# A fused decoder layer: the head norm's weights and residual on VectorE, the second norm and the choice of experts one or two tiles sooner

## What is computed

```python
x = _layernorm(x + _L0_attn_ref(x, ...))            # a state space scan
x = _layernorm(x + _L0_xattn_ref(x, ctx, ctx, ...)) # mLSTM, 4 heads of 64, queries from x, keys and values from ctx
x = _layernorm(x + _L0_ffn_ref(x, ...))             # 8 experts, each token uses 2
```

```python
h = jnp.einsum('bnst,bntd->bnsd', C / (normalizer + EPS_BACKEND), vh)
mean = h.mean(-1, keepdims=True)
var = h.var(-1, keepdims=True)
hn = (h - mean) * jax.lax.rsqrt(var + NORM_EPS) * outnorm_weight
# residual and layernorm, then:
logits = x @ gate_w
mult, sel = _sparse_mixer_routing(logits)   # the two best of 8 experts, and their gates
out = jnp.einsum('etf,efh,te->th', silu(x @ w1) * (x @ w3), w2, w)
```

## Time and profile before

| what | us |
|---|---|
| median of 3 runs (800.7 to 806.85) | 802.03 |
| the profiled execution | 804.1 |
| its span in the profile | 802.6 |
| TensorE busy | 678.2 (84%) |
| VectorE busy | 432.3 (54%) |
| ScalarE busy | 242.4 (30%) |
| GpSimd busy | 279.9 (35%) |

### The profile page before, as it was taken

One profiled execution on the slowest core, in us unless ns is written; L12 is line 12 of the kernel. 1 busy time (PEld: TensorE's weight loads), 2 busy tenths in 40 slices (PEclk: granted clock), 3 DMA queues, 4 the chain that ended last, 5 costly groups with the idle time before them and its releaser, 6 DMA issues.

```text
span 802.6 us, 13999 instructions
## 1 busy us (share of the span) xinstructions
PE 678.2 (84%) x3863; PEld 543.1 (68%) x3864; DVE 432.3 (54%) x1243; ACT 242.4 (30%) x473; POOL 279.9 (35%) x203
## 2 busy tenths in 40 slices
PE   6999879999957887843399999999999999999910
PEld 2566658887535665633288888888888888888810
DVE  3666673365435686797354454554445454455526
ACT  3444431111124844314032423223332323222204
POOL 7000010000102255766920272716463173710036
PEclk9998875599996977875599999999999999999965
DMA  9000017000210000412340004040414104000054
GB/s 288 14 0 2 0 49 162 1 0 1 112 46 1 1 2 0 178 57 90 120 185 27 26 26 183 26 183 26 183 33 183 33 27 183 26 28 27 26 181 146
DMA packets 33524, 57.88 MB, mean 72 GB/s; under 512 B 13328, under 2 KB 28432, under 8 KB 32208
## 3 DMA queue, kind: packets, MB, share of 16 engines
q1 hardware_dynamic: 24368, 42.88, 15.6%
q0 software_dynamic: 3360, 9.25, 3.2%
q10 hardware_dynamic: 5760, 5.33, 2.4%
HBM read 44.90 MB, written 12.54 MB: 72 GB/s over the span
## 4 chain that ended last, share of the span: by engine, by line
PE 70%; DVE 13%; POOL 6%; ACT 4%; issue 3%; DMA 2%; POOLq 0%; DVEq 0%; SPq 0%; ACTq 0%
PE bank L1944 25%; PE bank L1964 12%; PE bank L1634 6%; PE bank L1754 4%; PE bank L1954 4%; PE bank L1739 3%; POOL experts_w L760 3%; PE bank L1742 2%; PE bank L1644 2%; PE bank L1863 1%; DVE small L1205 1%; PE bank L1774 1%; PE bank L1824 1%; POOL small L647 1%; PE bank L1930 1%
## 5 line engine op out<-in xcount | busy, mean ns | idle before, releaser
L1944 PE MATMUL bank<-experts_w,experts_x 128*128 x912 | 231.1, 402 | 3.0 <-POOL experts_w L760 1.5
L1944 PEld LDWEIGHTS bank<-experts_w,experts_x 128*128 128x128 f32 x912 | 167.3, 190 | 39.3 <-issue 4.2
L1563 DVE TENSOR_TENSOR region<-region,bank 128x512 f32<-128x512 f32 x76 | 52.3, 688 | 171.7 <-ACT region L1003 171.7
L1964 PE MATMUL bank<-experts_w 128*128 x912 | 127.6, 289 | 1.9 <-DVE experts_w L1567 1.2
L1003 ACT ACTIVATE region<-bank 128x512 f32<-128x512 f32 x76 | 45.4, 597 | 246.2 <-PE bank L1944 246.1
L1964 PEld LDWEIGHTS bank<-experts_w 128*128 128x128 f32 x912 | 113.7, 191 | 2.3 <-issue 2.3
L771 POOL DMA_INDIRECT yrows<-region,rid x38 | 36.9, 972 | 203.4 <-DVE region L1577 191.3
L760 POOL TENSOR_TENSOR experts_w<-wstage,experts_w 128x3072 f32 x12 | 81.8, 6819 | 5.9 <-issue 5.9
L647 POOL TENSOR_TENSOR small<-small 128x4 f32<-128x4 f32 (+4 forms) x18 | 28.4, 1577 | 149.5 <-DVE small L1197 113.5
L1634 PE MATMUL bank<-xcol,region 128*128 128x512 f32 x128 | 58.9, 620 | 7.3 <-DMA xcol<-in_xT 7.3
L1567 DVE TENSOR_TENSOR experts_w<-bank,experts_w 128x512 fp32r<-128x512 f32 x76 | 51.9, 683 | 1.4 <-issue 1.4
(11 more groups left out here) (305 smaller groups left out, 1028.0 us busy)
## 6 DMA issues: line engine op xcount, KB each, us to landing
wstage<-in_w_exp SPq DMA_DIRECT2D x8, 3072.0 KB, 10.8
region<-slots ACTq DMA_DIRECT2D x40, 130.0 KB, 2.1
region<-yrows SPq DMA_DIRECT2D x8, 512.0 KB, 7.9
xcol<-in_xT SPq DMA_DIRECT2D x4, 512.0 KB, 7.3
xtok<-in_x SPq DMA_DIRECT2D x1, 2048.0 KB, 12.8
region<-in_ctxT SPq DMA_DIRECT2D x1, 2048.0 KB, 7.9
region<-in_ctx SPq DMA_DIRECT2D x4, 512.0 KB, 9.2
out<-xtok SPq DMA_DIRECT2D x4, 512.0 KB, 2.9
```

Of the source, the lines that this page charges most:

```text
L1563: dve.tensor_tensor(hmid[:, u], gsil[:, u], bank[2 * u + 1][:, :], ALU.mult).then_inc(mid_done, 1)
L1944: mm = pe.matmul(bank[2 * u + m][:, :], (xTh, xTl)[a][:, s, k, :], moving(off, w, m * KD * F + k * F + u * HALF, HALF), start=(k == 0 and ...
L1964: mm = pe.matmul(bank[6][:, 0:D], (hTh, hTl)[a][:, u, c, :], moving(off, w, 2 * KD * F + (4 * u + c) * D, D), start=(u == 0 and c == 0 and ...
```

## The change

The head norm's weights and residual move from GpSimd to VectorE for all batches: they stand right behind `head_apply` at c = 0. A batch's `norm2_stats` comes at c = 1 and not at c = 2, and `norm2_scale` and `norm2_apply` at c = 2 and not at c = 3. On ScalarE `norm2_apply` stands ahead of the second half of `weigh_keys`, where it used to stand behind it. The turning comes at the last tile of the batch that follows and not one tile later, the ranks one tile after it and not three tiles after. The choice of experts comes behind the next batch's `head_stats` at c = 3, and its placing at the next c = 0. GpSimd's list is rewritten: the low weights in two pieces of three parts, the scatters of a batch sooner and never between the `rsqrt`s of the last batch. In the tail VectorE chooses batch 2's experts before it applies the last batch's head norm. No other part of the program is touched.

```diff
--- before.py
+++ after.py
@@ -55,8 +55,8 @@
 HORNER = 10
 GATES_LAST = (B - 1) * NJ
 UNITS = tuple((NQ * b, NQ) for b in range(B - 1)) + ((NT - NQ, NQ - 1), (NT - 1, 1))
-TURN_AT = {NQ * (b + 2): b for b in range(B - 2)}
-RANK_AT = {i + 2: b for i, b in TURN_AT.items()}
+TURN_AT = {NQ * (b + 2) - 1: b for b in range(B - 2)}
+RANK_AT = {i + 1: b for i, b in TURN_AT.items()}
 KEEP = 4
 LO_PARTS = 12
 STATE_LIMIT, DECAY_LIMIT = 99.0, 80.0
@@ -666,14 +666,6 @@
                 ins = pool.tensor_tensor(kw[:, n], vaug[:, s, :, 0:DH], bc(fac[:, NQ - 1 + n, 0, :], 2, [P, H, DH]), ALU.mult)
             ins.then_inc(kw_done, 1)
 
-            def head_weights(u):
-                pool.wait_ge(heads_done, u + 1)
-                first, n = UNITS[u]
-                rows = hbuf[:, first % NQ:first % NQ + n].rearrange("p q h d -> p q (h d)")
-                here = xtok[:, first:first + n, 0:D]
-                link(pool.tensor_tensor(rows, rows, bc(onw[:, :], 1, [P, n, D]), ALU.mult))
-                pool.tensor_tensor(here, here, rows, ALU.add).then_inc(resid_done, 1)
-
             def scatter(tiles, g):
                 pool.wait_ge(row_done, g + 1)
                 for i in tiles:
@@ -689,30 +681,25 @@
                                        ALU.subtract).then_inc(w_lo, 1)
 
             rsqrt(NQ * H)
-            head_weights(0)
             rsqrt(NQ)
             pool.wait_ge(w_hi, 1)
-            low_weights(0, 2)
+            low_weights(0, 3)
             rsqrt(NQ * H)
-            head_weights(1)
-            low_weights(2, 2)
+            scatter(range(0, 2), 0)
             rsqrt(NQ)
-            low_weights(4, 2)
+            low_weights(3, 3)
             pool.wait_ge(w_lo, WPARTS)
             pool.sem_inc(w_ready, 1)
-            scatter(range(0, 1), 0)
             rsqrt(NQ * H)
-            head_weights(2)
-            scatter(range(1, 3), 0)
+            scatter(range(2, 4), 0)
+            scatter(range(4, 5), 1)
             rsqrt(NQ)
-            scatter(range(3, 4), 0)
+            scatter(range(5, 8), 1)
             late = UNITS[B - 1][1]
             rsqrt(late * H)
             rsqrt((NQ - late) * H, late * H)
-            scatter(range(NQ, 2 * NQ - 1), 1)
             rsqrt(late)
             rsqrt(NQ - late, late)
-            scatter(range(2 * NQ - 1, 2 * NQ), 1)
             scatter(range(2 * NQ, 3 * NQ), 2)
             scatter(range(3 * NQ, NT), 3)
             pool.wait_ge(w_hi, 2)
@@ -969,6 +956,8 @@
                     router_exp(RANK_AT[i])
                 if i in TURN_AT:
                     norm2_turned(TURN_AT[i])
+                if b and c == 2:
+                    norm2_apply(b - 1)
                 if b + 1 < B and c in (1, 2):
                     weigh_keys(b + 1, range(3 * c - 3, 3 * c))
                 if SPLIT_HI <= i < SPLIT_HI + WPARTS:
@@ -977,14 +966,12 @@
                     part = slice((i - SPLIT_HI) * WPART, (i - SPLIT_HI + 1) * WPART)
                     ins = act.copy(hi_of(slot_at[0])[:, part], wstage[:, part])
                     ins.then_inc(w_part if i < SPLIT_HI + WPARTS - 1 else w_hi, 1)
-                if b and c == NQ - 1:
-                    norm2_apply(b - 1)
             norm2_turned(B - 2)
+            router_exp(B - 2)
             for u in range(B - 1, len(UNITS)):
                 norm2_apply(u)
             for u in range(B - 1, len(UNITS)):
                 norm2_turned(u)
-            router_exp(B - 2)
             router_exp(B - 1)
 
             wait_filled(act, ("num", NT - 1))
@@ -1446,37 +1433,37 @@
                 if i + 1 < NT:
                     weights(i + 1)
                 else:
+                    head_stats(b)
+                if b and c == 2:
                     norm2_scale(b - 1)
-                    head_stats(b)
                 sums_of(i)
                 if b and c == 0:
-                    head_apply(b - 1)
-                if b >= 2 and c == 1:
-                    take_logits(b - 2)
-                    route_first(b - 2)
-                    route_second(b - 2)
-                    route_gates(b - 2)
-                if b and c == 2:
-                    norm2_stats(b - 1)
                     if b >= 2:
                         route_place(b - 2)
+                    head_apply(b - 1)
+                    head_weights(b - 1)
+                if b and c == 1:
+                    norm2_stats(b - 1)
                 if b < B - 1 and c == NQ - 1:
+                    head_stats(b)
                     if b:
-                        norm2_scale(b - 1)
-                    head_stats(b)
+                        take_logits(b - 1)
+                        route_first(b - 1)
+                        route_second(b - 1)
+                        route_gates(b - 1)
             head_stats(B)
+            take_logits(B - 2)
+            route_first(B - 2)
+            route_second(B - 2)
             for u in range(B - 1, len(UNITS)):
                 head_apply(u)
             for u in range(B - 1, len(UNITS)):
                 head_weights(u)
             for u in range(B - 1, len(UNITS)):
                 norm2_stats(u)
-            take_logits(B - 2)
-            route_first(B - 2)
+            route_gates(B - 2)
             for u in range(B - 1, len(UNITS)):
                 norm2_scale(u)
-            route_second(B - 2)
-            route_gates(B - 2)
             route_place(B - 2)
             for u in range(B - 1, len(UNITS)):
                 take_logits(u)
@@ -1910,9 +1897,9 @@
                     logits(TURN_AT[i])
             turn_norm2(B - 2)
             logits(B - 2)
-            turn_norm2(B - 1)
             ranks(B - 2)
-            turn_norm2(B)
+            for u in range(B - 1, len(UNITS)):
+                turn_norm2(u)
             for u in range(B - 1, len(UNITS)):
                 logits(u)
             ranks(B - 1)
```

## The result

The changed kernel is **slower**: 824.07 us (818.37 to 829.68, 4 runs) against 804.44 us (800.7 to 809.51, 4 runs) of the kernel before, ratio **1.0248 [1.0207, 1.0288]**. Run again beside the kernel before it gave 1.0216 [1.0168, 1.0264]. The forecast was 817 in a range of 800 to 824: right in direction, and 7 us short, so that the range just missed it. Some 5 us of the 7 are in the sum of its terms. The rest is that the profiled execution lay 2.1 above the median before, and only 0.4 now.

A forecast was written before the change was run, and what follows sets the result against it. Bound: a relay of waits between engines up to the last row, then TensorE. Terms 16.4 + 6.2 - 3.1 - 0.4 = +19.1, less 4.0 for the clock, +15.1: 819.2 from the profiled 804.1, 817 against the median; range 800 to 824.

The forecast's parts named there:

- What bounds the kernel: Up to the last row no engine is full; a relay of waits bounds it, with almost no slack in ScalarE's list.
- Term A: Batch 0 to batch 1, first heads instruction to values of tile 8: +16.4 us, at the least +8.8.
- The give-back for the clock: TensorE's clock recovers in part after the waits in batches 1 and 2: 4.0 us taken off the sum.
- term B: Batch 1 to batch 2, values of tile 8 to values of tile 12: +6.2 us, at the least -1.4.
- The hold in batch 1's norm: GpSimd's low_weights hold VectorE's copy and product of norm2_scale once together, 2.3 us, plus 0.3 for themselves.
- the rival to which I gave 0.07: Each of the two norm2_scale instructions is held by itself: 2.3 us more in both batches, 822 us; chance 0.07.
- Term C: From the values of tile 12 to the last row: 43.5 us where it was 46.65, so -3.1.
- The start: First heads instruction of batch 0, at 276.45 us, which nothing before it moves: change 0.
- D: Hand-over from the last row to the experts: shorter scatter queue, then padding writes are late next, -0.4 us.
- The expert stage started later and ended later by the same amount: Expert stage, bound by TensorE and left alone by the change, depends only on its start: own length changes by 0.
- The scatters end before the padding writes: Sign expected in the profile after, at the hand-over to the experts: the padding writes, landing at 391.1 before, end last.

The follow-up runs named there:

- The new tail by itself: Kernel before, with only the changed kernel's code behind the loop (choice of batch 2 ahead of the last heads, scatters sooner): 805.94 us, ratio 1.0005.
- keys first: Changed kernel, with ScalarE's second half of weigh_keys put ahead of norm2_apply again: 815.82 us, ratio 1.0035 to the kernel before.
- the filler: Changed kernel, with 12 and 24 unused constant matmuls in TensorE's waits ahead of the states of batches 2 and 3: 822.75 us, ratio 1.022.

## Why the prediction was right in direction and short in size

**What bounds the kernel, and where the change bites: right.** The place named was ScalarE's list. The keys behind `norm2_apply` and GpSimd's hold on `norm2_scale`, mended together, take the kernel back to 0.9995 of before.

**Term A: right** in its sum, +16.5 against +16.4, states 10.0 us later against 10.3, hold 2.30 against 2.3. One part of its working was wrong without harm: I had TensorE busy until 286.5 and idle for over 7 us; it waited 3.22 for sums first, and 4.78 for keys.

**The give-back for the clock: the first step that failed.** I took 4.0 us off because "the clock recovers in part", a quarter of 5.3 in term A and half of it in term B. No row stood behind these shares. In A nothing came back on the path: states, turning and values took the 9.0 us of the list. In B 1.9 came back, where I had 2.65. So the term was 2.1 us too large.

**The hold in batch 1's norm, in term B: the second.** I took one hold of 2.3 for copy and product, 2.6 with their own time. From the end of the root to the end of the product it was 4.6 (325.19 to 329.83), 2.31 and 2.37 by turns: the rival to which I gave 0.07, true in this norm only. Term B came out at +6.9 against +6.2 by luck, since these 2.0 us too few and the 1.9 that the clock gave back in the same loop nearly cancel.

**Term C: the third.** -1.3 against -3.1. The choice of batch 2 waits 1.84 us for its logits, a wait that I had put at nothing, and that is as much as the difference. How much C is worth hangs on the profile: the kernel before took 47.6, 50.1 and 52.8 us from the values of tile 12 to the last row in its three, the changed one 47.1 in both. The new tail by itself gave no gain.

These three are 2.1, 2.0 and 1.8 us. The start (-0.9), D (-0.6) and small pieces make 5.3 of them. With the three terms as measured the forecast is 823.

**The rest.** The expert stage started later and ended later by the same amount (408.8 us long, was 408.6). The scatters end before the padding writes, as forecast, and D is small.

## What to carry to other kernels

Before an instruction with a wait is moved up an engine's list, read what stands behind it and who waits for that: here 8.61 us of ScalarE's idle time stood in front of 2.96 us of keys that had been ready, and putting the keys first again brought the last row 8.0 us forward. Ask also which engine's long instructions start at the moment when a short one is released. When a relay is slowed by a wait, price what follows at the low clock, and keep the recovery for the range: the same work between states and values took 9.0 us once and 7.1 one batch later. And before filler is judged, look if it lasted as long as the wait.

## What the runs showed of the hardware

- A copy and a product of 4 numbers for each partition on VectorE, 0.17 and 0.16 us alone, are held either together (2.30 and 0.15) or one by one (2.31 and 2.37) by the same three GpSimd instructions of 2.3 us. Both profiles of the changed kernel, that of keys first and that with the filler show it so, together in batch 0 and one by one in batch 1. In the two of the changed kernel the product's record starts 0.02 us ahead of GpSimd's second in either case; what decides it stays open.
- SyncE's eight padding writes, with a register load each, took 8.8 to 9.2 us in seven profiles, 10.4 to 10.6 in six and 17.0 to 17.2 in two, all with the same code for them; the kernel before has both 8.88 and 17.01. The long ones go in steps of 0.69 us for the most part. The level changed between sets of runs, also between two on the same chip (8.76 to 9.24 in the second set, 17.01 in the fifth). Its cause is not known.
- Filler that ran at a clock of 1.00 and ended 2.98 us ahead of the states did not keep them off the low level (0.50).
- Behind a wait of TensorE for its keys the same states, turning and values took 9.0 us in one batch, at the low level, and 7.1 in the next, where the clock came back in the middle of the turning (the changed kernel, 293.03 to 302.01 and 334.85 to 341.91).
